# A decoder layer on one core: keys split during self-attention, another order in its step, and cross-attention with four-head sums and whole-pair weighing

## What is computed

```python
x = x + self_attn(layernorm(x))          # 32 heads of 16, 8 key groups, causal
x = x + cross_attn(layernorm(x), ctx)    # 8 heads x 4 batches, 64 rows each
x = x + ffn(layernorm(x))                # ternary weights, activations rounded to 8 bits
# cross_attn: q, k, v viewed as (32, 64, 512); k and v are both ctx
qk  = einsum('bdm,bdn->bmn', q, k) / 8;  ret = einsum('bmn,bcn->bcm', softmax(qk), v)
# ffn weights: clip(round(w / mean|w|), -1, 1)
```

## Time and profile before

| | us |
|---|---|
| median of 3 runs | 791.97 (790.47 to 792.49) |
| profiled execution | 791.34 |
| its span, first to last instruction | 789.5 |
| self-attention, from the trace | about 98 to 373.9 |
| output projection | 373.9 to about 437 |
| cross-attention | about 437 to 597 |
| FFN | about 597 to the end |

### The profile page before, as it was taken

One profiled execution on the slowest core, in us unless ns is written; L12 is line 12 of the kernel. 1 busy time (PEld: TensorE's weight loads), 2 busy tenths in 40 slices (PEclk: granted clock), 3 DMA queues, 4 the chain that ended last, 5 costly groups with the idle time before them and its releaser, 6 DMA issues.

```text
span 789.5 us, 15365 instructions
## 1 busy us (share of the span) xinstructions
PE 758.5 (96%) x4832; PEld 420.6 (53%) x4886; DVE 637.8 (81%) x1905; ACT 491.1 (62%) x844; POOL 423.1 (54%) x459
## 2 busy tenths in 40 slices
PE   8999999999999999998999899999998999999998
PEld 6777544444444444443777555555543455455543
DVE  7676888889888889881589878888977899888883
ACT  4665567667766776676355555555556576567564
POOL 5554489999999700000234367777886444423331
PEclk9999999999999999999899999999999999999999
DMA  8898674444544311200486434444420011000001
GB/s 289 301 385 282 210 186 136 122 132 133 139 128 130 96 54 52 61 18 3 146 284 236 162 108 136 134 136 135 121 70 18 11 42 41 28 15 27 28 26 42
DMA packets 65888, 94.79 MB, mean 120 GB/s; under 512 B 27184, under 2 KB 38576, under 8 KB 64272
## 3 DMA queue, kind: packets, MB, share of 16 engines
q1 hardware_dynamic: 61344, 80.77, 32.5%
q0 software_dynamic: 3952, 12.98, 5.8%
q10 hardware_dynamic: 512, 0.07, 0.1%
HBM read 72.88 MB, written 20.51 MB: 118 GB/s over the span
## 4 chain that ended last, share of the span: by engine, by line
PE 40%; DVE 5%; issue 3%; ACT 2%; POOL 1%; SPq 0%; DMA 0%; ACTq 0%; DVEq 0%; POOLq 0%
PE r_p L1698 12%; PE r_p L1633 7%; PE r_pn L1646 7%; PE r_p L1728 3%; PE r_pn L1728 3%; PE r_p L1605 3%; PE r_p L1661 2%; PE r_p L1712 2%; DVE r_stats L1384 1%; DVE tok L1403 1%; PE r_p L1587 1%; DVE r_xl L1397 1%; ACT r_xn L1235 1%; DVE r_mx L1416 0%; DVE r_h L1500 0%
## 5 line engine op out<-in xcount | busy, mean ns | idle before, releaser
L787 ACT ACTIVATE b_probs<-ab_j 128x512 f32<-128x512 f32 (+1 forms) x352 | 176.7, 560 | 25.5 <-PE ab_j L852 14.6
L148 DVE CUSTOM_DVE_ANT_0 b_junk<-ab_t,mask_qk 128x128 bf16<-128x128 f32 (+2 forms) x243 | 108.7, 485 | 27.0 <-PE ab_t L128 26.7
L852 PE MATMUL ab_j<-qs,ks 98*128 98x512 bf16 (+1 forms) x352 | 121.8, 361 | 2.9 <-DMA qs<-mrow 1.1
L1277 ACT ACTIVATE r_probs<-r_p 128x512 f32<-128x512 f32 x128 | 69.5, 599 | 65.2 <-PE r_p L1633 63.8
L148 DVE CUSTOM_DVE_ANT_0 b_junk<-ab_e,mask_qk 128x256 bf16<-128x256 f32 (+2 forms) x237 | 103.6, 482 | 0.3 <-issue 0.2
L1416 DVE TENSOR_REDUCE r_mx<-r_p 128x1 f32<-128x512 f32 x128 | 82.4, 675 | 22.1 <-PE r_p L1605 21.2
L1175 POOL TENSOR_TENSOR r_halves<-r_probs 128x1024 f32<-128x1024 f32 x32 | 76.6, 2395 | 34.8 <-DVE r_total L1446 24.9
L1327 ACT ACTIVATE r_silu<-r_p,r_cg 128x512 f32<-128x512 f32 x64 | 44.2, 691 | 53.0 <-PE r_p L1698 51.7
L870 PE MATMUL ab_pv<-b_probs,v 128*32 128x512 f32 (+3 forms) x1024 | 75.6, 436 | 0.0
L1202 POOL TENSOR_SCALAR r_h<-r_h,r_fh 128x1024 f32<-128x1024 f32 x32 | 38.0, 1199 | 64.8 <-DVE r_fh L1546 64.8
L128 PE MATMUL ab_e<-ks,qs 96*128 96x128 bf16 (+3 forms) x269 | 64.0, 300 | 5.3 <-DVE mx L148 0.7
(11 more groups left out here) (177 smaller groups left out, 1761.3 us busy)
## 6 DMA issues: line engine op xcount, KB each, us to landing
qs<-q_parts SPq DMA_DIRECT2D x32, 192.0 KB, 3.3
q_parts<-a_parts SPq DMA_DIRECT2D x15, 384.0 KB, 6.1
a_wst<-in_w_gate SPq DMA_DIRECT2D x4, 1024.0 KB, 7.7
a_wst<-in_w_up SPq DMA_DIRECT2D x4, 1024.0 KB, 9.9
a_wst<-in_w_down SPq DMA_DIRECT2D x4, 1024.0 KB, 8.3
qs<-q_parts SPq DMA_DIRECT2D x32, 128.0 KB, 3.2
b_wst<-in_w_gate POOLq DMA_DIRECT2D x16, 256.0 KB, 3.8
b_wst<-in_w_up POOLq DMA_DIRECT2D x16, 256.0 KB, 3.3
```

The source lines that it names most:

```text
L148: best = nc.vector.tensor_tensor_reduce(out=junk[:, 2 * (st.use[i, k] % slots) + n, 0:w], in0=bank[:, c:c + w], in1=keep["mask_qk"][:, SEQ ...
L787: nc.scalar.activation(pblock(j % 2, kb)[:, j0:j0 + nj, c:c + w], p2[(NE * j + n) % BANKS2][:, 0:nj * w].rearrange("p (j c) -> p j c", j=n ...
L852: last = nc.tensor.matmul(bank, ks[0:STACK + 2, s, kb * P:(kb + 1) * P], qs[0:STACK + 2, s, j0:j0 + nj, kb * P + c:kb * P + c + w], start= ...
L1277: nc.scalar.activation(probs[:, 2 * (p % 2) + a, blk, :], p2_bank("s", j, n)[:], ACT.Exp, scale=SCALE).then_inc(p2_used, 1)
```

## The change

Self-attention's order, in `Steps.order` and in `tensor` (weighing moves up behind the third unit of first scores, the turn of outputs down behind S(7)):

```diff
-        self.order = [0, 1, self.OUT, 2, self.TURN] + list(range(3, self.nu))
+        self.order = [0, 1, 2, self.TURN, 3, 4, 5, 6, 7, self.OUT, 8, 9]
...
-            F(0); S(0); F(1); S(1)
+            F(0); F(1); S(0); F(2)
+            W(0); W(1); W(2); W(3)
+            turn_maxima(nc, pe, st, keep, i)
+            S(1); F(3); S(2); S(3); F(4); F(5); S(4); S(5); F(6); F(7); S(6); S(7)
             turn_outputs()
...
+            S(8); F(8); S(9); F(9); S(10)
```

ACT copies `osb` after nine exponentials and not after five. The rounding of weights uses other operations, and when all 48 chunks are rounded POOL splits the keys, one pair a step, with ACT's copy at the end of steps 21 to 36 (`KEYS_FROM` is 37 - 16 = 21); both parts go to DRAM:

```diff
-            nc.gpsimd.tensor_scalar(out, raw, MAGIC, None, ALU.subtract).then_inc(wq2, 1)
+            nc.gpsimd.tensor_scalar(out, raw, MAGIC, 1.0, ALU.subtract, ALU.min).then_inc(wq2, 1)
             pool.wait_ge(wq2, t + 1)
-            nc.gpsimd.tensor_scalar(out, out, 1.0, -1.0, ALU.min, ALU.max)
+            nc.gpsimd.tensor_scalar(out, out, -1.0, 1.0, ALU.max, ALU.min)
...
+        def load_keys(p):
...
+            pool.dma_start(key_raw[:, p % 2, :], io["ctx"][P * p:P * (p + 1), :]).then_inc(key_in[p % 2], 16)
+        def split_keys(p):
+            pool.wait_ge(key_high, QUANTISED + p + 1)
...
+            nc.gpsimd.tensor_tensor(key_l[...], key_raw[...], key_h[...], ALU.subtract).then_inc(key_low, 1)
+            pool.wait_ge(key_low, QUANTISED + p + 1)
+            for name, tile in (("kh", key_h), ("kl", key_l)):
+                pool.dma_start(scr[name][P * p:P * (p + 1), :], tile[:, p % 2, :].bitcast(F32)).then_inc(key_out[p % 2], 16)
+        pool.wait_ge(wq2, QUANTISED)
+        load_keys(0)
+        load_keys(1)
+        for p in range(KPAIRS):
+            split_keys(p)
+            load_keys(p + 2)
+        for s in range(2):
+            pool.wait_ge(key_out[s], 32 * (KPAIRS // 2))
...
+            p = i - KEYS_FROM                      # scalar(act), at the end of step i
+            if 0 <= p < KPAIRS:
+                act.wait_ge(key_in[p % 2], LOADED + 16 * (p // 2 + 1))
...
+                nc.scalar.activation(key_h[:, p % 2, :], key_raw[:, p % 2, :], ACT.Copy).then_inc(key_high, 1)
```

In the second block ACT's copy (1246) and DVE's subtraction (1428) are gone, and SP loads both parts, in iterations 2p-1 (high) and 2p+2 (low). Weighing and sums:

```diff
-            p = pair_due(i, 8)
-            if p is not None and p < LATE_SUMS:
-                sum_probs(p)
-            p = pair_due(i, 5)
-            if p is not None:
-                weigh(p, 0)
-                weigh(p, 1)
+            q = quad_due(i, 10)                    # i = 4q+10
+            if q is not None and q < QUADS - 1:
+                sum_probs(q)
             p = pair_due(i, 6)                     # i = 2p+6
             if p is not None:
-                weigh(p, 2)
-                weigh(p, 3)
+                for nb in range(KD):
+                    weigh(p, nb)
...
-                for a in range(2):
-                    last = nc.tensor.matmul(p2_bank("sum", p)[a * H:(a + 1) * H, :], keep["ones64"][:], total[:, 2 * (p % 2) + a, :], start=True, stop=True)
+                for a in range(4):
+                    last = nc.tensor.matmul(p2_bank("sum", q)[a * PART:(a + 1) * PART, :], keep["ones64"][:, 0:PART], total[:, (4 * q + a) % TSLOTS, :],
+                                            start=True, stop=True)
```

More of the change, by code:

```diff
@@ L789, in exponential @@
                                      ACT.Exp, scale=float(HDIM) ** -0.5).then_inc(exps, 1)
-            for n in range(5):
+            for n in range(9):
                 exponential(n)
@@ L797, in scalar @@
                 nc.scalar.activation(osb[:, j3 % 2, :], pv[:], ACT.Copy).then_inc(osb_full, 1)
-            for n in range(5, NE):
+            for n in range(9, NE):
                 exponential(n)
+            p = i - KEYS_FROM
+            if 0 <= p < KPAIRS:
+                act.wait_ge(key_in[p % 2], LOADED + 16 * (p // 2 + 1))
+                if due(32 * (p // 2)):
+                    act.wait_ge(key_out[p % 2], 32 * (p // 2))
+                nc.scalar.activation(key_h[:, p % 2, :], key_raw[:, p % 2, :], ACT.Copy).then_inc(key_high, 1)
     def vector(dve):
@@ L1002, in rest_of_layer @@
                     p2_use["s", i - 4, n] = len(p2_use)
-            if i >= 8 and i % 2 == 0 and (i - 8) // 2 < PAIRS:
-                p2_use["sum", (i - 8) // 2] = len(p2_use)
+            if i >= 10 and (i - 10) % 4 == 0 and (i - 10) // 4 < QUADS:
+                p2_use["sum", (i - 10) // 4] = len(p2_use)
         P1_USES, P2_USES = len(p1_use), p2_use["s", HEADS_X - 1, STEP - 1] + 1
-        LATE_SUMS, LAST_SUM_BODY = PAIRS - 2, E_FIRST + 2
+        LAST_SUM_BODY = E_FIRST + 2
         def p1_bank(*key):
@@ L1011, in p2_bank @@
         def p2_bank(*key):
-            return p2[SBANKS - 1] if key[0] == "sum" and key[1] >= LATE_SUMS else p2[p2_use[key] % SBANKS]
+            return p2[SBANKS - 1] if key == ("sum", QUADS - 1) else p2[p2_use[key] % SBANKS]
         def pair_due(i, behind):
@@ L1017, in pair_due, with quad_due, load_keys, load_keys_low @@
             return s // 2 if s >= 0 and s % 2 == 0 and s < HEADS_X else None
+        def quad_due(i, behind):
+            s = i - behind
+            return s // 4 if s >= 0 and s % 4 == 0 and s < HEADS_X else None
         @block.sync
         def _(sp):
-            def load_context_rows(p):
-                sp.dma_start(k2[:, p % 2, :], io["ctx"][P * p:P * (p + 1), :]).then_inc(k_in[p % 2], 16)
+            def load_keys(p):
+                if p >= 2:
+                    sp.wait_ge(k_in[p % 2], 16 * (p // 2))
+                if due(STEP * 2 * (p - UNROLL + 1)):
+                    sp.wait_ge(scores, STEP * 2 * (p - UNROLL + 1))
+                sp.dma_start(kh[:, p % UNROLL, :].bitcast(F32), scr["kh"][P * p:P * (p + 1), :]).then_inc(k_in[p % 2], 16)
+            def load_keys_low(p):
+                if due(STEP * 2 * (p - 1)):
+                    sp.wait_ge(scores, STEP * 2 * (p - 1))
+                sp.dma_start(kl[:, p % 2, :].bitcast(F32), scr["kl"][P * p:P * (p + 1), :]).then_inc(kl_in[p % 2], 16)
             def load_query_rows(p):
@@ L1087, in attend_context @@
                     load_query_low(p)
+                p = pair_due(i, 2)
+                if p is not None and p >= 2:
+                    load_keys_low(p)
                 p = pair_due(i, 3)
@@ L1649, in weigh, with sum_probs @@
                     last.then_inc(weighted, 1)
[L1651 to L1656 removed]
+            def sum_probs(q):
+                pe.wait_ge(first_total, 2 * q + 2)
+                pe.wait_ge(second_total, 2 * q + 2)
+                if q < QUADS - 1:
+                    pe.wait_ge(p2_used, p2_use["sum", q] - SBANKS + 1)
+                else:
                     pe.wait_ge(p2_used, P2_USES)
[L1658 to L1661 removed]
+                for a in range(4):
+                    last = nc.tensor.matmul(p2_bank("sum", q)[a * PART:(a + 1) * PART, :], keep["ones64"][:, 0:PART], total[:, (4 * q + a) % TSLOTS, :],
+                                            start=True, stop=True)
                 last.then_inc(summed, 1)
@@ L1721, in down @@
                         elif j == 1:
[L1722 removed]
+                            pe.wait_ge(p2_used, p2_use["sum", QUADS - 1] + 1)
                         else:
```

194 lines of the change are left out of this document (87 added, 107 removed).

## The result

The changed kernel takes 897.6 us (median of 4 runs, 896.8 to 898.7) against 791.2 for the kernel before beside it (788.7 to 792.5): a ratio of 1.135, 95% interval 1.132 to 1.138. The forecast was 785.9 with a range of 776 to 799: wrong in sign, and far outside. The profiled execution has a span of 895.3 us where it was 789.5; its mean granted clock is 0.924, where it was 0.994.

What follows compares the result with a forecast made beforehand. PE was taken as the bound, losing time to DVE's late banks in self-attention and dense in cross-attention. -13 + 11.6 - 0.5 - 4.6 + 0.5 = -6.0 took the span from 789.5 to 783.5; median 785.9, range 776 to 799.

Steps and rivals of the forecast that it cites:

- the rounding's: POOL's rounding of weights: line 760 falls from 1.49 to 0.62 us, a chunk takes 2.66, done near 231.
- Rival 1: POOL's rounding stays slow, line 760 at 1.49; ACT and PE stand 15.5 us for a key: 801 us; chance 0.17.
- The seam: Between self-attention's end and the second block: the last keys lie open, +11.6 us (9.6 to 13.7).
- rival 4: No added time between self-attention and the second block: 774 us; chance 0.03.
- T + 15.9: Forecast start of the second block, T being the end of self-attention's last exponentials; T + 4.3 before.
- Self-attention's order: New order of PE's work in a self-attention step: period 8.25 us for 8.73, together -13 us (-16 to -4).
- Output projection: Two ACT copies and a DVE subtraction go: -0.5 us, between -1.5 and 0.
- Cross-attention: Sums and weighing regrouped: -14.3 us, +10.4 of stalls, -0.7 at i = 25; net -4.6 (-15 to +2).
- the sum: Cross-attention's sums on PE: 16 of 0.85 us become 8 of the same length, -6.8.
- boundaries: Cross-attention, PE going between kinds of product: weighing in one group saves 16 of 0.47 us, -7.5.
- the late stalls: Cross-attention from i = 18 to 32: PE waits 0.8 us for DVE's maxima in 8 even iterations.
- FFN: More products and additions beside feed bodies, a longer wait at the first turn of tokens: +0.5 us (0 to 2).

Runs made afterwards that it cites:

- old_round: The changed kernel with the two rounding lines of the kernel before; 814.5 us, ratio 1.0307 to the kernel before.
- prices: The kernel before with a different pair of rounding operations on POOL for each of the three weights, to price them; ran once, no total time given.
- fast_round: The changed kernel with weights rounded by (mult,add) then (min,max); 794.2 us, ratio 1.0056 to the kernel before.
- order_only: The kernel before with only the new order of the self-attention step, osb copied after nine exponentials; 776.9 us, ratio 0.9833.
- two_keys: fast_round with keys split two a step in self-attention steps 19 to 26, not one a step until 33; 773.3 us, ratio 0.9792 to the kernel before.
- moved: two_keys with DVE's product, reciprocal and second-tile moments moved out of odd cross-attention iterations, ACT's copy behind its fourth exponential; 765.0 us, ratio 0.9679 to the kernel before.
- split_weigh: two_keys with cross-attention's weighing of a pair cut in two again, sums by four heads kept; 767.3 us, ratio 0.9702 to the kernel before.
- late_dma: order_only plus one 256 KB load issued and waited for by POOL after the last weighing; 784.4 us, ratio 0.9922 to the kernel before.

## Why the prediction was wrong

**The step that failed** is the rounding's: "The ends are 0.6 and 1.5; I take 0.62, as all long two-operation forms on POOL are near it, and leave 762 as it is though its pair of operations changes." The trace of before has two pairs on POOL in its long forms, (mult,add) and (min,max); the forecast took them for all, and gave a reordered pair the old one's 0.61 in half a sentence. ("Near it" was loose besides: with f32 out, (mult,add) takes 0.70 in line 758 and 0.90 in line 1190 of that trace.) Both new pairs cost 1.92, which is outside even the upper end of 1.5. A chunk was 5.27 and not 2.66, POOL was done at 356.8 and not near 231, and ACT's key load, taken to be there 29 us early, held the stage for 99.9 us. The warning stood in the same rows: if one operation takes 2.4 times as long as a pair, the count does not set the price, and an unseen pair is unknown, for line 762 too.

**Rival 1** had the mechanism (POOL late, ACT at the key load, PE behind it, the deciding point of 256 us), at 0.17; its price of 15.5 was that of old_round's kind, where the wait measured 18.8 (a step of 27.03 for 8.23), and not the 99.9 of two lines at 1.92. The Trainium skill's GPSIMD Engine Reference, section 3.1, says that bodies of up to two operations an element are bound by the port. These runs do not bear it out for this instruction: at one or two operations the same shape took 0.61, 1.49 or 1.92 us.

**The seam** was right in kind, as rival 4's absence of one is refuted, and 8.3 short: T + 15.9 ended at the landing and the block is left only after POOL's drain. The row of it stood in the trace of before, 4.73 us long and hidden. "The block is left together" was the place to ask what leaving costs each engine. The rest of the seam came out as laid out, with the last store issued by 470.9 and landed at 473.2. And the lower clock behind the gap, 2.2 us, was no term at all. The profiled execution of before had the lower clock in the same place (67.9 from the block's start to iteration 5, for 65.3 in prices, the same code there), which hid it in the comparison of spans.

**Self-attention's order** was right: 8.23 for 8.25, -14.3 by fast_round's last `osb` copy (357.30 for 371.56) for -13. Rows of starts laid out by hand were enough, and order_only bears it out alone (-14.8).

**Output projection**: with the full clock behind the seam two_keys is at iteration 5 after 63.4 where order_only takes 65.4: -2.0 for -0.5, outside the bounds of -1.5 to 0. By the last product of the projection it is -1.6. What brings more than forecast was not looked into.

**Cross-attention**: -4.6 forecast, and between -0.9 (fast_round: 58.6 + 70.9 + 24.8 = 154.3 for 63.1 + 69.6 + 22.6 = 155.3, unrounded 155.2) and +0.2 (the changed kernel, 155.5, with 1.5 of the lower clock in it) measured from i = 5 to the FFN. The mechanism was right (odd 2.42, DVE's product in the way, PE waiting for the maxima), its terms less so: the sum 0.99 and not 0.85 (16 x 0.85 - 8 x 0.99: -5.7 for -6.8), boundaries 0.38 and not 0.47 (-6.1 for -7.5), and the late stalls 0.6 to 1.0 for 0.8, as the reciprocal, in every second odd iteration, was left out of DVE's list. Up to i = 32 the stalls came to 8.2 (two_keys against moved), for 9.6. With these terms, and the 0.7 of i = 25, it would still be -4.3. The rest is mainly the tail, where the forecast had 0.9 of stalls and otherwise its full savings: from i = 31 to the FFN it is 27.2 for 27.1, where split_weigh, which saves the sums alone, takes 25.0. PE's wait of 2.23 ahead of the turn of tokens was in no term.

**FFN**: -0.4 for +0.5, just outside its bounds of 0 to 2.

## What to carry to other kernels

A two-operation form on GpSimd is priced by its very pair: look for a row with those operations in that order, measure if there is none, and write rounding and clipping with pairs that are known fast. When a block ends with GpSimd's own transfers, its DRAIN comes after the last landing and grows with every transfer it has issued in the block; do that work early, where it is covered. When work on the bounding engine is bunched, the short iterations that are left must still hold what the other engines do in them: move that too, or the gain is given back. Before comparing two stretches that differ by a microsecond or two, look at the granted clock of both, and start and end them where both kernels have done the same work.

## What the runs showed of the hardware that was not expected

- GpSimd, 128x512 with bf16 out: (mult,add) and (min,max) 0.61 us, each of five single operations 1.49, each of seven other pairs 1.92. To write (max,min) for (min,max) costs 1.3 us an instruction.
- GpSimd's DRAIN took 82 to 83 ns per transfer that it had issued since the block began (50, 97 and 98 transfers: 4.15, 7.99, 8.08 us), with 4 KB as with 256 KB, though all had landed; on the other engines, SP with its transfers among them, it is 0.37 to 0.70.
- Behind gaps of PE the granted clock was at the lower level for 5 to 8 us after work resumed: 97 us idle (changed, until 360.9; low until 366.2), 21 us (changed, until 481.5; low until 489.1; fast_round, until 379.5; low until 385.6), 7 us (late_dma, until 366.1; low until 371.8).
- The same code had a stretch at the lower level in one profiled run and none in another (the tail of cross-attention: two_keys, 3.4 us, and fast_round, none). 3.4 us of it cost 1.5 there, and 1.7 in moved.
